# Loads of the first two routed tiles issued in the attention stage, and the routed stage's tiles moved in SBUF

## What is computed

```python
x = x + xattn(layernorm(x), ctx, ctx)          # 8 x 512 x 256
u = layernorm(x)
def expert(W1, b1, W2, b2):                    # 256 -> 1024 -> 256
    return gelu(rmsnorm(u) * g @ W1 + b1) @ W2 + b2
h_s = expert(shared 0) + expert(shared 1)
scores = sigmoid(u @ centroids)                # 8 experts
gk, i = top_k(scores, 2); gk = gk / scores.sum(-1)
h_r = sum over k of gk[k] * expert(routed i[k])
out = x + u + h_s + h_r
```

## The kernel before

| tiles | before | after |
|---|---|---|
| whi, wlo (routed) | 64 | 0 |
| xhi, xlo, hhi, hlo (routed) | 96 | 64 |
| raw (routed) | 64 | 32 |
| xt_0, xt_1 | 0, 32 | 32, 32 |
| whs, wls (shared) | 0 | 64 |
| xhs, xls, shared_hhi, shared_hlo | 96 | 32 |
| qcT | 0 | 32 |
| big (masked queries; spare rows) | 96 | 32, 32 |

## Time and profile before

### The profile page before, as it was taken

How to read it: one execution, slowest core, us unless ns; L and a number is a source line. 1 busy time by engine, 2 the same in 40 slices (tenths; PEclk the granted TensorE clock), 3 DMA queues, 4 the chain that set the end, 5 groups by cost and what they waited for, 6 DMA issues and landing times. The chain is left out here.

```text
span 1381.6 us, 21915 instructions
## 1 busy us (share of the span) xinstructions
PE 1166.5 (84%) x7861; PEld 1016.1 (74%) x7861; DVE 962.2 (70%) x2367; ACT 805.1 (58%) x1390; POOL 347.3 (25%) x319
## 2 busy tenths in 40 slices
PE   1544698797897897897987988779999999999996
PEld 1323476576676676676775777679999999999996
DVE  3674569568568667676686466178888888888883
ACT  1312355445554553553554434379999999999994
POOL 5302142041041041131221202013333333333332
PEclk9765799999999999999999997879999999999998
DMA  5010000000001011011000102088888888888882
GB/s 169 8 34 27 16 32 31 31 32 31 32 32 50 13 62 32 13 50 31 28 20 16 40 4 106 27 268 229 226 229 226 221 211 230 217 219 223 225 229 24
DMA packets 141774, 136.15 MB, mean 99 GB/s; under 512 B 48682, under 2 KB 127668, under 8 KB 141668
## 3 DMA queue, kind: packets, MB, share of 16 engines
q1 hardware_dynamic: 122948, 111.68, 25.7%
q0 software_dynamic: 14304, 18.75, 8.2%
q10 hardware_dynamic: 4416, 4.34, 0.9%
HBM read 109.42 MB, written 25.33 MB: 98 GB/s over the span
## 5 line engine op out<-in xcount | busy, mean ns | idle before, releaser
L1284 DVE TENSOR_TENSOR wlo<-raw,whi 128x512 fp32r<-128x512 f32 x312 | 219.7, 716 | 20.8 <-ACT whi L1237 16.7
L529 ACT ACTIVATE shared_hraw<-bank,b1s 128x512 f32<-128x512 f32 x128 | 88.2, 689 | 193.3 <-PE bank L1037 180.8
L1237 ACT CAST whi<-raw 128x512 fp32r<-128x512 f32 x312 | 191.6, 616 | 15.1 <-DMA raw<-in_L_ffn_W_r_dram 15.1
L1020 PE MATMUL bank<-whs,shared_hhi 128*128 128x256 f32 x512 | 150.2, 293 | 50.0 <-DVE shared_hlo L755 50.0
L1209 PE MATMUL bank<-xhi,whi 128*128 128x256 f32 x624 | 176.0, 282 | 6.9 <-DVE wlo L1284 6.9
L1189 PE MATMUL bank<-whi,hhi 128*128 128x256 f32 x624 | 179.7, 288 | 0.0
L1189 PE MATMUL bank<-whi,hlo 128*128 128x256 f32 x624 | 176.4, 283 | 0.0
L1209 PE MATMUL bank<-xlo,whi 128*128 128x256 f32 x624 | 176.3, 283 | 0.0
L1209 PE MATMUL bank<-xhi,wlo 128*128 128x256 f32 x624 | 176.1, 282 | 0.0
L755 DVE TENSOR_TENSOR shared_hlo<-shared_hraw,shared_hhi 128x512 fp32r<-128x512 f32 x128 | 89.9, 706 | 122.4 <-ACT shared_hhi L532 119.4
L1189 PE MATMUL bank<-wlo,hhi 128*128 128x256 f32 x624 | 175.0, 281 | 0.0
(11 more groups left out here) (263 smaller groups left out, 2697.9 us busy)
## 6 DMA issues: line engine op xcount, KB each, us to landing
raw<-in_L_ffn_W_r_dram SPq DMA_DIRECT2D x78, 1024.0 KB, 5.4
xt<-sorted_tokens SPq DMA_DIRECT2D x39, 260.0 KB, 2.8
xb<-in_x_dram SPq DMA_DIRECT2D x8, 512.0 KB, 4.3
cb<-in_ctx_dram SPq DMA_DIRECT2D x8, 512.0 KB, 3.7
xr<-in_x_dram SPq DMA_DIRECT2D x8, 512.0 KB, 3.5
out_dram<-base ACTq DMA_DIRECT2D x8, 512.0 KB, 3.1
sorted_tokens<-chunk SPq DMA_DIRECT2D x9, 260.0 KB
out_dram<-yt,token POOLq DMA_INDIRECT x78, 4.0
```

The costliest lines, as they stand in the source:

```text
L529: nc.scalar.activation(hraw[:, k % NHB, :], up_bank[k % 2][:, :], ACT.Gelu, bias=b1s[:, k // M, k % M:k % M + 1]).then_inc(gelu_done, 1)
L1020: last = mm(down_bank[j // 2][:, (j % 2) * D:(j % 2 + 1) * D], h[:, k % NHB, j * P:(j + 1) * P], w[:, e, wsl], start=k == 0 and t == 0 and ...
L1237: nc.scalar.copy(whi[i][:, psl], raw[i][:, psl]).then_inc(t_whi, 1)
L1284: nc.vector.tensor_tensor(wlo[i][:, psl], raw[i][:, psl], whi[i][:, psl].bitcast(fp32), ALU.subtract).then_inc(t_wlo, 1)
```

## The change

The two raw buffers become the attention stage's `big` tiles, and the two xt buffers lie in its `qcT`; both, with the b1 buffers, are now allocated on `whole`. The eight loads of tiles 0 and 1 are issued at the end of SyncE's program of the attention stage, behind the fills, after waits for all scatters and for a new semaphore `tables_known`, which VectorE raises at the end of `tables()`. SyncE's program of the routed stage starts with g_r's column and goes on with tile 2. A tile `room` of 32 bytes is added between padf and xT. No computation is changed.

```diff
@@ -72,6 +72,35 @@
         tile_at = sb(whole, "tile_at", [P, NT], i32)
         pad_token = sb(whole, "pad_token", [P, NT, TJ])
         owner_no = sb(whole, "owner_no", [P, NT])
+        WN = KD * HID
+        big = [sb(whole, "big_0", [P, 2 * WN]), sb(whole, "big_1", [P, 2 * WN])]
+        qcT = sb(whole, "qcT", [P, 2 * KD, S])
+        raw = big
+        xt = [qcT[:, KD * i:KD * i + KD, :].rearrange("p k s -> p (k s)")[:, 0:TJ * XW].rearrange("p (j d) -> p j d", d=XW)
+              for i in range(2)]
+        b1 = [sb(whole, f"b1_{i}", [P, M]) for i in range(2)]
+        t_x = [sem(f"t_x{i}") for i in range(2)]
+        t_w1 = [sem(f"t_w1{i}") for i in range(2)]
+        t_w2 = [sem(f"t_w2{i}") for i in range(2)]
+        t_b1 = [sem(f"t_b1{i}") for i in range(2)]
+        w1_v = W1_r.rearrange("e (k p) h -> e p k h", p=P)
+        w2_v = W2_r.rearrange("e (m p) d -> e p m d", p=P)
+        b1_v = b1_r.rearrange("e (m p) -> e p m", p=P)
+
+        def tile_loads(sp, n, first, second):
+
+            i = n % 2
+            e = sp.value_load(tile_expert[0:1, n:n + 1], min_val=0, max_val=NE - 1)
+            at = sp.value_load(tile_at[0:1, n:n + 1], min_val=0, max_val=NE * RR)
+            first()
+            sp.dma_start(xt[i][:, :, :], xs_v[bass.ds(at, 1)].rearrange("n p j d -> (n p) j d")).then_inc(t_x[i], 16)
+            sp.dma_start(raw[i][:, 0:WN].rearrange("p (k h) -> p k h", k=KD),
+                         w1_v[bass.ds(e, 1)].rearrange("e p k h -> (e p) k h")).then_inc(t_w1[i], 16)
+            sp.dma_start(raw[i][:, WN:2 * WN].rearrange("p (m d) -> p m d", m=M),
+                         w2_v[bass.ds(e, 1)].rearrange("e p m d -> (e p) m d")).then_inc(t_w2[i], 16)
+            second()
+            with nc.allow_non_contiguous_dma(reason="a bias column per hidden chunk"):
+                sp.dma_start(b1[i][:, :], b1_v[bass.ds(e, 1)].rearrange("e p m -> (e p) m")).then_inc(t_b1[i], 16)
 
 
         stage_a = ExitStack()
@@ -90,12 +119,10 @@
         lnsc = A("lnsc", [P, D])
         gs_col = A("gs_col", [P, KD])
         cent = A("cent", [P, KD, NE])
-        WN = KD * HID
         whs = A("whs", [P, NS, 2 * WN], fp32r)
         wls = A("wls", [P, NS, 2 * WN], fp32r)
         b1s = A("b1s", [P, NS, M])
         eps = A("eps", [P, 2])
-        big = [A("big_0", [P, 2 * WN]), A("big_1", [P, 2 * WN])]
         spare = big[1][0:KE, :].bitcast(bf16)
         exp_rhs = spare[:, 0:J * NH * P].rearrange("p (j h s) -> p j h s", j=J, h=NH)
         head16 = spare[:, J * NH * P:J * NH * P + S]
@@ -115,7 +142,6 @@
         xb = A("xb", [P, J, D])
         cb = A("cb", [P, J, D])
         qn = A("qn", [P, J, D])
-        qcT = A("qcT", [P, 2 * KD, S])
         qmask = big[0][:, :].rearrange("p (g r s) -> p g r s", g=KD, r=HG)
 
         norm_x, norm_u = ((A(f"bn6_{n}", [P, J, 6]), A(f"mv_{n}", [P, J, 2]), A(f"nw_{n}", [P, 5, J])) for n in "xu")
@@ -301,7 +327,7 @@
                         sc.dma_start(fg_bias[FG + r * NH:FG + (r + 1) * NH, :], fg_b.rearrange("(h o) -> h o", o=1)
                                      ).then_inc(s_gate, 16)
 
-        s_zero, ends_known = sem("s_zero"), sem("ends_at_ready")
+        s_zero, ends_known, tables_known = sem("s_zero"), sem("ends_at_ready"), sem("tables_known")
         s_fill, s_scat, s_base_out = sem("s_fill"), sem("s_scat"), sem("s_base_out")
         s_b2 = sem("s_b2")
         minus_exp, chain_r, picked, counted, counts_read = (
@@ -416,6 +442,10 @@
                     at = sp.value_load(ends_at[0:1, e:e + 1], min_val=e * REGION, max_val=e * REGION + CAP)
                     sp.dma_start(xs_dram[bass.ds(at, T), :].rearrange("(p j) d -> p j d", j=TJ), zeros).then_inc(s_fill, 16)
                 sp.wait_ge(s_fill, 16 * (NE + 1))
+                sp.wait_ge(s_scat, 16 * TOPK * J * B)
+                sp.wait_ge(tables_known, 1)
+                for n in range(2):
+                    tile_loads(sp, n, lambda: None, lambda: None)
 
             @block.gpsimd
             def _(pool):
@@ -888,6 +918,7 @@
                         own.done(tt(begun, owner, least[:, h:h + 1, :].to_broadcast([P, NT, NE]), ALU.mult))
                         own.done(nc.vector.tensor_reduce(pad_token[:, :, h], begun, AX.X, ALU.add))
                     own.end()
+                    dve.sem_inc(tables_known, 1)
 
                 passes(dve, {"front": front, "back": back, "unit": unit, "hand_over": hand_over, "split": split,
                              "base": to_add, "finish": finish, "route": route})
@@ -1092,15 +1123,13 @@
         PIECE = 2 * WN // M
         NP1 = WN // PIECE
         gr_col = Cc("gr_col", [P, KD])
-        raw = [Cc(f"raw_{i}", [P, 2 * WN]) for i in range(2)]
         whi = [Cc(f"whi_{i}", [P, 2 * WN], fp32r) for i in range(2)]
         wlo = [Cc(f"wlo_{i}", [P, 2 * WN], fp32r) for i in range(2)]
-        b1 = [Cc(f"b1_{i}", [P, M]) for i in range(2)]
-        xt = [Cc(f"xt_{i}", [P, TJ, XW]) for i in range(2)]
         NG = 4
         gate = [Cc(f"gate_{i}", [P, TJ]) for i in range(NG)]
         token = [Cc(f"token_{i}", [P, TJ], i32) for i in range(NG)]
         padf = Cc("padf", [P, TJ])
+        Cc("room", [P, 8])
         xT = Cc("xT", [P, KD, T])
         xhi = [Cc(f"xhi_{i}", [P, KD, T], fp32r) for i in range(2)]
         xlo = [Cc(f"xlo_{i}", [P, KD, T], fp32r) for i in range(2)]
@@ -1109,18 +1138,11 @@
         hlo = Cc("hlo", [P, NHB, T], fp32r)
         yt = [Cc(f"yt_{i}", [P, TJ, D]) for i in range(2)]
         s_gr = sem("s_gr")
-        t_x = [sem(f"t_x{i}") for i in range(2)]
-        t_w1 = [sem(f"t_w1{i}") for i in range(2)]
-        t_w2 = [sem(f"t_w2{i}") for i in range(2)]
-        t_b1 = [sem(f"t_b1{i}") for i in range(2)]
         t_whi, t_wlo = sem("t_whi"), sem("t_wlo")
         t_tr, t_xraw, t_xhi, t_xlo = sem("t_tr"), sem("t_xraw"), sem("t_xhi"), sem("t_xlo")
         t_up, t_gelu, t_hhi, t_hlo, t_step = (sem(n) for n in ("t_up", "t_gelu", "t_hhi", "t_hlo", "t_step"))
         t_y = sem("t_y")
         t_meta, t_own, t_acc = sem("t_meta"), sem("t_own"), sem("t_acc")
-        w1_v = W1_r.rearrange("e (k p) h -> e p k h", p=P)
-        w2_v = W2_r.rearrange("e (m p) d -> e p m d", p=P)
-        b1_v = b1_r.rearrange("e (m p) -> e p m", p=P)
         YB = TJ * D // 512
         NU = 4 // YB
         y_bank = [psum[NU + i * YB:NU + (i + 1) * YB] for i in range(2)]
@@ -1142,25 +1164,15 @@
                 with nc.allow_non_contiguous_dma(reason="a column per half"):
                     sp.dma_start(gr_col[:, :], g_r.rearrange("(k p) -> p k", p=P)).then_inc(s_gr, 16)
 
-                def body(n, i, r):
-                    e = sp.value_load(tile_expert[0:1, n:n + 1], min_val=0, max_val=NE - 1)
-                    at = sp.value_load(tile_at[0:1, n:n + 1], min_val=0, max_val=NE * RR)
-                    if n > 1:
-
+                def body(n):
+                    def free():
                         sp.wait_ge(t_wlo, M * (n - 1))
                         sp.wait_ge(t_tr, n - 1)
                         sp.wait_ge(t_meta, n - 1)
-                    sp.dma_start(xt[i][:, :, :], xs_v[bass.ds(at, 1)].rearrange("n p j d -> (n p) j d")).then_inc(t_x[i], 16)
-                    sp.dma_start(raw[i][:, 0:WN].rearrange("p (k h) -> p k h", k=KD),
-                                 w1_v[bass.ds(e, 1)].rearrange("e p k h -> (e p) k h")).then_inc(t_w1[i], 16)
-                    sp.dma_start(raw[i][:, WN:2 * WN].rearrange("p (m d) -> p m d", m=M),
-                                 w2_v[bass.ds(e, 1)].rearrange("e p m d -> (e p) m d")).then_inc(t_w2[i], 16)
-                    if n > 1:
-                        sp.wait_ge(t_gelu, M * (n - 1))
-                    with nc.allow_non_contiguous_dma(reason="a bias column per hidden chunk"):
-                        sp.dma_start(b1[i][:, :], b1_v[bass.ds(e, 1)].rearrange("e p m -> (e p) m")).then_inc(t_b1[i], 16)
-                for n in range(NT):
-                    body(n, n % 2, n // 2)
+
+                    tile_loads(sp, n, free, lambda: sp.wait_ge(t_gelu, M * (n - 1)))
+                for n in range(2, NT):
+                    body(n)
 
             @block.tensor
             def _(pe):
```

## The result

| | before | after |
|---|---|---|
| time, median of the runs on one chip (us) | 1380.43 (1378.24 to 1383.44, 4 runs) | 1364.34 (1363.36 to 1369.19, 4 runs) |
| profiled execution, time / span (us) | 1384.11 / 1381.6 | 1369.19 / 1367.5 |
| last attention matmul to first routed matmul, line 1209, now 1221 (us) | 15.70 | 11.86 |
| tile 0 / tile 1 (us) | 12.89 / 13.45 | 13.02 / 11.70 |
| a routed tile, mean of 20 (us) | 11.81 | 11.61 |

The ratio is 0.9889, with a 95% interval of 0.9859 to 0.9919: against 1380.4 us that is 15.3 us less (11.2 to 19.5). Against the forecast's own base, 1380.26, it makes 1364.9 us, where 1376.7 was predicted with a range from 1365.0 to 1380.5. The direction held; the likeliest case was out by a factor of four, and the time lies at the lower edge of the range.

A forecast was written before the change was run, and what follows sets the result against it. It took TensorE's matmuls to bound the routed stage, after a 15 us gap between stages. Terms: 3.6 us for early loads plus 0 for tile places, 1380.26 - 3.6 = 1376.7 us, range 1365 to 1380.5.

The forecast's parts named there:

- the first rival: Routed matmuls fall to the attention stage's pace, weights then on multiples of 128: 1369 us (1366 to 1372), chance 0.27.
- the plain case: Likeliest outcome: 3.6 us between the stages, 0 from tile places, 1376.7 us (1375.1 to 1378.3), chance 0.43.
- The hand-over: Between attention and routed stages: loads of tiles 0 and 1 issued early bring the first routed matmul 3.6 us forward.
- The bounds (2.9 to 4.5): Gain between the stages: 4.5 us if g_r's column landed at once, 2.9 if it or the barrier came late.
- the 0 for the places: Routed matmuls: moving operands by 32 bytes to multiples of 64 changes their pace by 0 us; far bound 41 us.
- signs of being wrong: Tiles of 11.5 us or below, changed spacing of lines 1020 or 1037, ScalarE waiting for raw, changed tile 1 length.
- The 5 us that this rival feared: Attention stage, line 1020: whs and wls moving off 128 by 64 could give back up to 5 us.
- Both operands on 64 as a regime of its own: Routed matmuls run faster with both operands on multiples of 64: about 1347 us (1336 to 1356), chance 0.08.
- The estimate from the Trainium skill's: Routed matmuls at 109.2 ns per 256 columns if alignment were the reason: 34 us less, 1343 us.
- The slower case: Routed stage: transfers into raw, 32 past 64, slow down: 1384.5 us at 21% more per write, chance 0.07.
- The half-clock stretch in tile 1: Second stretch at half clock, after tile 0's end stall; its change taken as 0, with 1.6 us either way.

The follow-up runs named there:

- gr_early: Changed kernel with g_r's column also loaded in the attention stage, nothing else; ratio 0.9911 against the kernel before.
- d128: Kernel before, loads late, all routed TensorE operands on multiples of 128 bytes, weights and x/h 128 apart; one execution, 1383.3 us.
- w0_x96_h96: Kernel before, loads late, routed weights moved to multiples of 128, x and h tiles left 96 past one; one execution, 1374.4 us.
- w64_x64_h64: Kernel before, loads late, weights left 64 past a multiple of 128, x and h tiles moved to 64 past; one execution, 1380.2 us.
- changed_again: The changed kernel unaltered, run again beside the others; 1366.3 us, ratio 0.9899 against the kernel before.
- place_only: Kernel before, loads late, only the routed stage's TensorE tiles moved to their places in the changed kernel by 128; 1370.8 us, ratio 0.9944.
- all_off_64: Kernel before, loads late, every routed matmul operand moved off multiples of 64, at distance 192; one execution, 1369.6 us.
- x0_h64: Kernel before, loads late, routed tokens at distance 0 from the weights and h at distance 64; one execution, 1384.8 us.
- early_same_distance: Kernel before with the early loads, tiles padded to keep distance 160 in the routed stage; 1375.3 us against 1380.6, ratio 0.9965.
- best: Changed kernel with g_r's column loaded early, hhi and hlo moved 128 bytes, attention distances set the same way; 1369.3 us, ratio 0.9915.
- early_only: Kernel before with the early loads, TensorE operands padded to their old places by 128, distance 32; 1373.9 us against 1376.2, ratio 0.9975.
- plus256: Changed kernel with 72 instead of 8 elements of room, x and h 256 bytes further from the weights; one execution, 1371.7 us.

## Why the prediction was wrong where it was

The range reached down to 1365.0 for the sake of the first rival, whose reason didn't hold (below). That the time came out at its edge is luck, and not the mechanism of the plain case.

**The hand-over was right.** It said eight issues on SyncE between 862 and 870, transposes within 1 us of the block's start, VectorE's first read as g_r lands, and the first matmul 12 us behind the last of attention, 3.6 us less. SyncE's queue in the changed kernel:

```profile
863.34 0.41 SPq L96 DMA_DIRECT2D qcT<-sorted_tokens  x1
...
871.11 1.29 SPq L103 DMA_DIRECT2D b<-in_L_ffn_b_r_dram  x1
892.36 0.38 SPq L1165 DMA_DIRECT2D gr_col<-in_L_ffn_g_routed_dram  x1
```

Eight issues from 863.34 to 871.11, then 20 us of nothing. The gap is 11.86 to 11.88 us in the five profiles with early loads and the late column, whatever their places, and 3.8 us shorter than before. The bounds (2.9 to 4.5) held, and gr_early showed what is late next.

**The step that failed is the 0 for the places**, "the pace hardly knows of 32 bytes ... because the two nearest rows are exactly alike". They were alike, 0.456 ns per column both, but they were the wrong pair. Lines 1020 and 1037 have their misplaced operand on opposite sides, so they answer whether the misplaced *stream* costs more than the misplaced *stationary* operand. They lie at the same distance, 224, and so do the same two lines after the change: the comparison held fixed the one thing that counts, and no row of before varied it in the same line. The routed stage's own pair was not alike, 0.70 and 0.72 us for six, and the 0 passed over that. Measured: 38 x 0.197 = 7.5 us. Of the prediction's signs of being wrong, tiles of 11.5 us or below didn't come, but line 1189 did gain more than 1209: 2.7 ns (119.5 to 116.8) and 1.3 (117.3 to 116.0).

**The rival that came nearest in size had another reason.** "The routed matmuls fall to the attention stage's pace" gave 1369, from 1.6 ns a matmul, and the means fell to 116.0 and 116.8 ns, from 118.3. Its observation was sound: line 1189 at 120 ns, line 1020 at 116.7, the same form. But its reason was that the attention weights lie on multiples of 128. d128 has that and gains nothing. What the two stages differ in is their distance, 160 and 224, and w0_x96_h96 shows line 1189 at 116.9 ns once it has the attention stage's. The 5 us that this rival feared in the attention stage, since whs and wls move off 128, didn't come: everything there moves together, and its spacing is 1.41 and 1.40 us per group as before.

**Both operands on 64 as a regime of its own** (1347) falls with w64_x64_h64, 11.947 us, the slowest. The estimate from the Trainium skill's "TensorE: Matmul & The Clock Gate", section "Wait — 56ns, not 53.3ns?", 109.2 ns for 256 columns, was not reached by this form in any kernel. Over tiles 5 to 35 the shortest spacing in any of the fourteen profiles is 112 ns, and in the changed kernel the single matmuls go from 113 to 122.

**The slower case** (raw misplaced) didn't come either. In the changed kernel, with raw 32 past 64, no engine waited for a load from tile 2 on, and the casts that read raw took 615 ns, 616 before. The median time from issue to landing of the routed weights is 5.4 us before and 7.3 in this profile, but that isn't the place of raw: changed_again, the same kernel, has 5.5, and place_only, with raw where it was before, 7.3. The page on the DMA issues:

```profile
big<-in_L_ffn_W_r_dram SPq DMA_DIRECT2D x78, 1024.0 KB, 7.3
```

**The half-clock stretch in tile 1** was priced at 0 with 1.6 us to either side, and 1.75 of the 14.1 us of the two profiled executions are this. All fourteen profiles have a wait at the end of tile 0, as in the earlier trace rows. What tells them apart is when full clock first came in tile 0: the first two matmuls, the transposes of tile 1 among them, that start 0.10 to 0.15 us apart, counted from the first routed matmul.

| full clock after (us) | kernels | half-clock stretch in tile 1 |
|---|---|---|
| 3.52, 3.53, 3.97, 3.98, 4.13 | gr_early, all_off_64, x0_h64, d128, before | in all five |
| 4.56, 4.57, 5.25, 5.26, 5.63, 5.65 | early_same_distance, changed_again, best, place_only, w0_x96_h96, w64_x64_h64 | in none |
| 6.20, 6.21, 6.22 | early_only, plus256, after | in none |

Where full clock comes early, TensorE reaches the missing low half sooner, and its wait is longer: 1.87 to 2.25 us in the first row, 1.11 to 1.79 in the others. So this is one order of events seen fourteen times, a long wait and then the lower clock; that the wait is the cause wasn't tried. The profiles after and changed_again are of one kernel and have full clock 1.65 us apart, so chance has a part in it. Whether the early loads shift the odds stays open: the stretch is there in four of the seven profiles with late loads, in none of the five with early loads and the late column, and in one of the two with the early column.

**The sum, with what is known now:** 3.8 for the loads and 7.5 for the places make 11.3 us, 1369.0 against 1380.26. By time, the parts measured alone make 4.8 + 7.7 = 12.5, and the whole 15.3 and 13.9 in the two sets of runs. 11.3 lies at the lower edge of both intervals (11.2 to 19.5 and 11.3 to 16.7). I can't name what the 2 to 4 us above it are, if they are more than chance; fewer half-clock stretches would be worth up to 1.75. Time and trace part by as much elsewhere, and either way: early_only gained 3.4 us by time and 7.1 by the trace, best 11.7 and 4.6 + 3.3 = 7.9. So the times bear out the two parts, but not the sum to a few us.

**What stays open.** Why the distance counts. A clash between the load of one stationary operand and the stream of another, in SBUF, would fit: it needs both addresses, repeats in them, and two lines side by side could then act on each other, as x0_h64 and best show. But this is argued and not shown. That each 256 columns take 0.21 us at half clock whatever the distance only says that there is room then. I left out what would show it, a kernel with nothing in it but two tiles and a swept distance. The Trainium skill's page "SBUF — State Buffer", section "Specifications (TRN2)", gives cachelines of 16 bytes and a penalty for each crossing to a new line. All starts here are multiples of 32 bytes, so lines alone tell none of these kernels from another, and the measured 11.61 to 11.95 us a tile need something else.

## What to carry to other kernels

When two rows agree, ask what they hold fixed: they bound only what differs between them, and a thing that no row varies has no bound of 0. For back-to-back fp32r matmuls with a weight load each, the start of stationary and streamed tiles relative to one another is worth a sweep in steps of 32 bytes up to 256, since a few unused elements moved a tile by 2.8% here; alignment by itself was worth nothing. And a change that does two things should be measured with each alone, with all else held, addresses included: my first try at "the loads alone" had moved the pace as well.

## What the runs showed of the hardware that I had not expected

- The pace of fp32r matmuls (128x256 streamed, a new stationary operand each) follows the distance between the two operands' tiles by its rest in 256 bytes: 11.95 us a tile at 0, 11.72 at 32, 11.61 at 64 and 192, 11.81 to 11.82 at 128 and 160, 11.74 at 224. Adding 256 at distance 64 changes nothing (11.613 both); adding 128 to distance 32 does (11.723 and 11.820). The distance of the neighbouring line counts too (x0_h64, best).
- The start by 64 or 128 bytes has no effect that shows: 11.622 us a tile with all on 64 and 11.625 with all off it, at distance 192; 11.814 with all on 128, at distance 128.
- The spacing isn't even, except at distance 0 (nine in ten are 120 ns). In the changed kernel stretches of 113 to 114 ns alternate with some of 116 to 122, and a tile's pace is their mix.
- A stationary and a streamed operand can be exchanged if the distance's sign is too: 116.0 ns for up at 64 and for down at 192.
- After the waits of 1.87 to 2.25 us on TensorE at the end of tile 0 the granted clock fell to 1.2 GHz for a part of tile 1 (five profiles of five); after those of 1.11 to 1.79 us it stayed at 2.4 GHz (nine of nine).
